# Softmax attention on TensorE: in each half slot, the pair of scores for maxima issued ahead of the pair of transposed scores

## The reference, cut to what matters

```
mixed = x @ Wqkv.T                       # 16 heads of 16 channels
attn  = softmax(q @ k.T / sqrt(16))      # per batch and head, 512 x 512
ctx   = attn @ v
out   = ctx @ Wproj.T + bproj            # added to x
```

## Time and profile before

| | us |
|---|---|
| median of 3 runs | 1160.34 (1159.0 to 1160.65) |
| the profiled execution | 1158.43 |
| its span | 1156.6 |
| PE busy in the span | 1120.4 (97%) |
| DVE busy | 938.7 (81%) |
| ACT busy | 763.3 (66%) |
| POOL busy | 627.9 (54%) |

### The profile page before, as it was taken

How to read it: one execution, slowest core, us unless ns; L and a number is a source line. 1 busy time by engine, 2 the same in 40 slices (tenths; PEclk the granted TensorE clock), 3 DMA queues, 4 the chain that set the end, 5 groups by cost and what they waited for, 6 DMA issues and landing times. The chain is left out here.

```text
span 1156.6 us, 22545 instructions
## 1 busy us (share of the span) xinstructions
PE 1120.4 (97%) x7600; PEld 906.2 (78%) x7600; DVE 938.7 (81%) x2140; ACT 763.3 (66%) x1527; POOL 627.9 (54%) x1070
## 2 busy tenths in 40 slices
PE   8999999998998999999999999999999999999988
PEld 7444444346767899999999999999999999999866
DVE  6889887866569888888888888888888888888972
ACT  3467677773437767676777777677777767676633
POOL 4020500001715876877786786777687677767620
PEclk9999999999999999999999999999999999999999
DMA  6333333301221112111111201210210211110120
GB/s 187 56 56 57 56 56 57 56 2 38 81 71 37 36 33 85 33 49 70 48 33 37 81 33 49 70 48 33 81 37 33 83 35 49 34 48 34 33 73 1
DMA packets 23450, 60.51 MB, mean 52 GB/s; under 512 B 3367, under 2 KB 8359, under 8 KB 22183
## 3 DMA queue, kind: packets, MB, share of 16 engines
q1 hardware_dynamic: 23335, 59.07, 18.9%
HBM read 44.67 MB, written 2.33 MB: 41 GB/s over the span
## 5 line engine op out<-in xcount | busy, mean ns | idle before, releaser
L1830 DVE SCALAR_TENSOR_TENSOR ln_xn<-l_proj_q,par,ln_xn 128x511 f32<-128x511 f32 (+2 forms) x192 | 142.3, 741 | 96.6 <-ACT ln_xn L1712 94.3
L781 DVE TENSOR_REDUCE a_neg_max<-a_scores 128x1 f32<-128x512 f32 x244 | 154.6, 681 | 29.0 <-PE a_scores L437 27.2
L679 ACT ACTIVATE a_probs<-a_scores_t 128x512 f32<-128x512 f32 x256 | 137.2, 598 | 50.1 <-PE a_scores_t L459 48.0
L96 POOL TENSOR_SCALAR ln_var_eps<-ln_mean_var 128x4 f32<-128x4 f32 (+1 forms) x13 | 3.0, 230 | 284.0 <-DVE ln_mean_var L86 193.3
L1718 ACT ACTIVATE ln_xn<-ln_xn,par 128x512 f32<-128x512 f32 x128 | 92.7, 724 | 92.0 <-DVE ln_xn L1830 92.0
L1417 POOL TENSOR_TENSOR l_k_tok<-l_normed,k_norm 128x384 f32<-128x384 f32 x63 | 64.1, 1017 | 153.5 <-ACT l_normed L1729 153.5
L1830 DVE SCALAR_TENSOR_TENSOR ln_xn<-l_proj_k,par,ln_xn 128x511 f32<-128x511 f32 (+2 forms) x192 | 142.8, 744 | 4.5
L1729 ACT ACTIVATE l_normed<-l_turn_q,l_shift,l_scale 128x128 f32<-128x128 f32 x252 | 94.7, 456 | 20.5 <-POOL l_shift L1410 20.3
L1408 POOL TENSOR_TENSOR l_scale<-l_small,l_minus_half 128x8 f32<-128x8 f32 x64 | 105.0, 1641 | 5.0
L1729 ACT ACTIVATE l_normed<-l_turn_k,l_shift,l_scale 128x128 f32<-128x128 f32 x252 | 95.6, 480 | 0.0
L1788 ACT ACTIVATE l_gate<-l_proj_gv 128x512 f32<-128x512 f32 x64 | 38.2, 597 | 81.6 <-PE l_proj_gv L1495 81.6
(11 more groups left out here) (395 smaller groups left out, 3522.6 us busy)
## 6 DMA issues: line engine op xcount, KB each, us to landing
l_keep<-keep_rows SPq DMA_DIRECT2D x64, 448.0 KB, 3.5
a_stack<-a_dense SPq DMA_DIRECT2D x90, 128.0 KB, 4.4
head_raw<-w_heads SPq DMA_DIRECT2D x8, 1024.0 KB, 6.7
x_tok<-x SPq DMA_DIRECT2D x4, 512.0 KB, 8.1
wo_raw<-w_o SPq DMA_DIRECT2D x1, 2048.0 KB, 11.4
out<-x_tok SPq DMA_DIRECT2D x1, 1920.0 KB
a_stack<-a_max_rows_t SPq DMA_DIRECT2D x64, 4.0 KB
ctx_tok<-w_qkv SPq DMA_DIRECT2D x1, 768.0 KB, 6.6
```

The lines of the kernel that those rows point to most:

```text
L679: act.activation(probs[:, n % 2, h, :], scores_t[(4 * n + h) % TURNS][:], ACT.Exp, scale=SOFT_SCALE).then_inc(probs_done, 1)
L781: dve.tensor_reduce(neg_max[:, g % 2, at:at + 1], max_bank(g, j), AX.X, ALU.max, negate=True).then_inc(max_done, 1)
L1830: ins = dve.scalar_tensor_tensor(conv[:, w, m, s:], proj[w][:, 0:SEQ - s], par[:, h, tap:tap + 1], conv[:, w, m, s:], ALU.mult, ALU.add)
```

## The change

The order in which PE issues the two pairs of a half slot is exchanged. No instruction is added, removed or altered; all semaphores and their counts stay. Where a slot has only one of the two kinds (slots 0 to 5 have no P, slots 64 to 69 no M), nothing changes but the place of the filler matmuls in slot 6, which come with P.

```diff
                 for half in range(2):
-                    if n >= 0:
-                        probs_chunk(n // chunks, n % chunks, half)
                     if s < groups:
                         for e in range(2):
                             max_scores(s, c * max_per_chunk + 2 * half + e)
+                    if n >= 0:
+                        probs_chunk(n // chunks, n % chunks, half)
                     if half == 0:
                         if n >= 1:
                             context(n - 1)
```

## The result

The changed kernel takes 1171.24 us (median of 4 runs, 1169.58 to 1172.46), the kernel before 1159.68 (4 runs), a ratio of 1.0098 with a 95% interval of 1.008 to 1.0117. It is 11.6 us slower where 7.1 were forecast. The profiled execution took 1172.46 us, its span is 1170.7; that is 14.0 us over the profiled execution of the kernel before, more than the medians differ.

The account below looks back on a forecast made before the run. No engine was taken as saturated; chains beginning at a P or an M release what PE waits for. Terms of 1.41 + 2.94 + 1.30 + 0.94 + 0.39 + 0.14 = 7.1 us on 1160.34 gave 1167.4, own range 1165 to 1170, whole 1162.8 to 1171.5.

Parts of the forecast that it names:

- larger: Rival: every context waits, or every half's exponentials come on the path; 13.6 us, 1174 us, chance 0.08.
- How far a pair moves: All exchanged pairs: a pair occupies 0.235 us, so P's exponentials start 0.235 later and the maxima 0.235 earlier.
- (a): Projection in c = 2, groups 1 to 6: its chain begins at P01, so it starts 0.235 later; 1.41 us.
- (b): c = 3 into c = 4, groups 1 to 6: maxima 0.235 later, P01 behind blocked M01 0.255 more; 2.94 us.
- (c): c = 7 into c = 0, groups 0, 2, 4: late maxima and P01 behind blocked M01, less 0.17 in slot 9; 1.30 us.
- (d): Context bank, slots 55, 59, 63 and 64: P23, exponentials, copy and C 0.235 later; 0.94 us.
- (e): c = 6 of groups 1, 3, 5: projection after ACT's copies of v, 0.10 slack covers part; 0.39 us.
- (f): c = 6 of groups 2 and 4: M01 fills P01's 0.17 us DMA wait, transposition only 0.07 later; 0.14 us.
- (g): DMA waits of P01 in slots 54, 58, 62: M01 goes ahead, but its second matmul waits; taken as 0.
- (h): C everywhere else: needs 2.9 us from one to the next, closest slots stand at 2.94; no loss.
- The drop at 326 us: Granted clock falls once near 326 us, mean 0.57 over 4 us; some 1.7 us that may come or go.
- a sign of being wrong: Loop: the prediction is wrong if the loss sits in slots its list leaves out, above all odd c; no size.

Follow-up runs that it names:

- c = 2 and 3 alone: Kernel before, with M01 ahead of P01 only in slots with c = 2 and 3: five runs 1165.69 to 1166.07 us, two 1160.54 and 1160.85.
- c = 0 and 4 alone: Kernel before, with M01 ahead of P01 only in slots with c = 0 and 4: ten runs from 1160.29 to 1168.53 us.
- the filler kernel: Changed kernel with M01's first matmul repeated 2 to 6 times in slots with c = 0 or 4, groups 1 to 6: 1166.78 us.
- P01 back in its place: Changed kernel, but P01 ahead of M01 again in slots with c = 0 and 4: median 9.4 us over the kernel before.
- the second half alone: Kernel before, with only M23 and P23 exchanged in each slot: loop 2.6 us longer apart from the clock.
- the early low part: Kernel before, with ACT's high part ahead of P01's exponentials and DVE's low part between M01's maxima, in c = 2 and some c = 6: 1156.13 us.
- the first half alone: Kernel before, with only P01 and M01 exchanged in each slot: 1175.23 us.

## Why the prediction was right or wrong

The direction was right, and so were the steps of the mechanism; a second mechanism was missing. The size was short by 4.5 us, of which nearly all is that one thing. The median of 1171.24 lies above the forecast's own 1165 to 1170 and within the whole range, up to 1171.5, by 0.3 us only. That upper part was there for the "larger" rival, so that it held is luck.

- *How far a pair moves*: right. P01 stands 0.33 to 0.34 behind M01, the chains are 0.24 later.
- *(a), projection in c = 2*: +0.22 to +0.24, six times; shown by the run with c = 2 and 3 alone and by cutting the chain.
- *(b), c = 3 into 4*: +0.47 at full clock as forecast. C came 0.67 behind the blocked M against 0.675 forecast. Shown by the same run and by that with c = 0 and 4 alone.
- *(c), c = 7 into 0*: +0.46 to +0.48 in groups 0, 2, 4, and 0 behind odd groups, as forecast. The 0.17 expected back in slot 9 didn't come.
- *(d)*: +0.22 to +0.24 in the four slots, and gone when the second half isn't exchanged.
- *(e)*: +0.14, three times, as forecast.
- *(f)*: wrong, +0.24 instead of 0.07. The wait of 0.17 us put down to a DMA in the earlier trace rows is no wait: after the change the same 0.17 stands there, now put down to DVE ahead of M01, and P01 waits for no DMA. It is the distance from the transpositions to the next pair (from first start to first start 0.58 before, 0.59 after).
- *(g), (h)*: nothing, as forecast; slot 56 stays 2.94 behind slot 55.
- *The drop at 326 us*, which might have come or gone: it stayed, 3.4 us long, at 338 us.

These sum to 7.5 us in the loop against 7.1 forecast, and the filler kernel, at full clock in its profiled loop, shows just that. The prediction gave as a sign of being wrong a loss in slots outside its list, above all those of odd c: 5.7 of the 13.2 us are of that kind, most of them in slots 13, 14 and 29.

**What failed** is the term that isn't in the sum. The prediction had the granted clock only at 326 us, as something that may come or go. It had no term for what (b) does to PE: it called the second P01 held behind the blocked M "0.255 more" and didn't ask how long PE then stands idle in one piece. In slots 12 and 28 that is 1.63 us where it was 0.23 and 0.59. The clock fell to half behind them, 5.7 us in the profiled execution and some 4.5 in the medians (1171.24 against 1166.78 with fillers). That PE's idle time there has a part in the drop is shown by the fillers, which take it away and the drop with it. Whether it is the one long piece or the sum of the pieces that counts, the fillers can't tell, since they shorten both. Which idle time brings a drop and which not stays open: pieces of 1.10 us were followed by one in two kernels and not at the same places in the changed one, and the clock also fell with P01 back in its place (0.60 us), with c = 2 and 3 alone (0.80), with the second half alone (0.45) and behind the very pieces of the kernel before (0.59, the early low part). The kernel before has executions with less clock as well. The rival "larger" gave 1174, a nearby time for a reason that didn't occur.

## What to carry to other kernels

When two streams share an engine that takes its work in order, look for which one stands at the head of the longest chain back to that engine, and keep it ahead. Before moving something behind an instruction that will block, ask also how long the engine then idles: on TensorE added idle time can cost more than its own length, here 4.3 us of halved clock in slots 12 to 14 for 0.8 us more of it. Look at the granted clock of every execution, since one profile shows only one of them. And a wait inside the loop was better cut in the middle of its chain here, in the queues of the engines that pass it on, than by pulling its first link forward.

## What the runs showed of the hardware

- In the profiled executions the granted clock halved for 3.4 or 10.2 us behind each slot in which PE had idled 1.33 to 1.63 us in one piece (the changed kernel, the first half alone, c = 0 and 4 alone). It also halved, for 3.4 to 10.2 us, behind longest pieces of 0.45 to 1.11 us in six kernels, while other pieces of 1.10 us had no drop behind them. It does not halve in every execution: the runs with c = 2 and 3 alone lie 5 us apart by it.
- Two half-height matmuls of 512 columns in different rows of the array start within 0.01 us, and such pairs follow each other 0.24 us apart (205.55 to 205.79 before); a pair between full-height matmuls costs about 0.52 (0.75 less 0.23).
- A short idle time of PE's weight loads right after transpositions (0.17 us here) is named after whatever released last, and needn't be a wait at all.
